# A graph-attention kernel: VectorE weights two gathered rows in two operations instead of one, and four products of TensorE's softmax chain get another form

## The reference

```python
def _gatv2_layer(x, src, dst, n, Wl, Wr, att, b):        # layers 0 and 1, with one self loop per node
    xl = (x @ Wl).reshape(n, H, C)
    xr = (x @ Wr).reshape(n, H, C)
    e = jax.nn.leaky_relu(xl[src] + xr[dst], NEG_SLOPE)
    logits = jnp.einsum('ehc,hc->eh', e, att)
    m = jax.ops.segment_max(logits, dst, num_segments=n)
    ex = jnp.exp(logits - m[dst])
    denom = jax.ops.segment_sum(ex, dst, num_segments=n)
    alpha = ex / (denom[dst] + 1e-16)
    msg = xl[src] * alpha[:, :, None]
    out = jax.ops.segment_sum(msg, dst, num_segments=n)
    return out.reshape(n, H * C) + b
...
    e = jax.nn.leaky_relu(s1[:, src] + s2[:, dst], ALPHA)   # layer 2: one score per node and head
    seg_max = jax.vmap(lambda x: jax.ops.segment_max(x, dst, num_segments=N))(e)
    ex = jnp.exp(e - seg_max[:, dst])
...
x = _layernorm(x + _L0_gnn_ref(...), axis=-1)
x = _layernorm(x + _L1_gnn_ref(...), axis=-1)
```

## Time and profile before

| | |
|---|---|
| median of three runs | 4111.03 us (4109.16 to 4114.46) |
| the profiled execution | 4120.86 us, its span 4119.0 us |
| mean granted TensorE clock | 0.948 |
| PE busy | 3664.7 us (89%), 31817 instructions |
| DVE busy | 3151.0 us (76%), 8749 instructions |
| POOL busy | 2738.6 us (66%), 2941 instructions |
| ACT busy | 1229.3 us (30%), 4200 instructions |
| L1558, the weighting | 1248 instructions, 856.2 us |
| L692, the gathers | 2496 instructions, 2545.3 us |

### The profile page before, as it was taken

How to read it: one execution, slowest core, us unless ns; L and a number is a source line. 1 busy time by engine, 2 the same in 40 slices (tenths; PEclk the granted TensorE clock), 3 DMA queues, 4 the chain that set the end, 5 groups by cost and what they waited for, 6 DMA issues and landing times. The chain is left out here.

```text
span 4119.0 us, 121901 instructions
## 1 busy us (share of the span) xinstructions
PE 3664.7 (89%) x31817; PEld 2727.4 (66%) x31818; DVE 3151.0 (76%) x8749; ACT 1229.3 (30%) x4200; POOL 2738.6 (66%) x2941
## 2 busy tenths in 40 slices
PE   6699999999999898999999999977788877887785
PEld 5577777777776676777777777745455555555553
DVE  6767877788778665788787787875688878887886
ACT  4433333333333563333333333323110111111113
POOL 5577777777775127777777777723777777777760
PEclk9899999999999999999999999989798888888889
DMA  4354444444443225444444444435555544544544
GB/s 98 108 141 130 132 131 132 126 133 131 131 126 98 62 66 136 134 131 132 126 133 131 130 128 133 125 107 177 137 135 138 139 132 136 138 136 132 137 107 125
DMA packets 333900, 521.05 MB, mean 126 GB/s; under 512 B 152888, under 2 KB 219618, under 8 KB 333810
## 3 DMA queue, kind: packets, MB, share of 16 engines
q0 software_dynamic: 120320, 338.39, 29.9%
q1 hardware_dynamic: 213489, 181.58, 15.5%
HBM read 484.14 MB, written 35.46 MB: 126 GB/s over the span
## 5 line engine op out<-in xcount | busy, mean ns | idle before, releaser
L692 POOL DMA_INDIRECT gathered<-table,idx x2496 | 2545.3, 1020 | 864.4 <-issue 519.3
L1131 PE MATMUL pS<-gathered,Dm 128*128 128x264 f32 x4992 | 1712.2, 426 | 92.8 <-DVE Dm L1541 48.3
L1528 DVE TENSOR_TENSOR acc_mem<-acc_mem,pS 128x264 f32 x2496 | 1039.6, 417 | 133.0 <-PE pS L1131 111.8
L1068 PEld LDWEIGHTS pZ<-DT,x 128*128 x9984 | 868.6, 99 | 338.3 <-issue 60.3
L1068 PE MATMUL pZ<-DT,x 128*128 128x128 bf16 x9984 | 1083.3, 221 | 10.4 <-DVE DT L1488 8.8
L853 ACT ACTIVATE reluT<-pZ 128x256 f32<-128x256 f32 x1664 | 637.0, 383 | 1301.4 <-PE pZ L1074 1283.2
L1131 PEld LDWEIGHTS pS<-gathered,Dm 128*128 128x128 f32 x4992 | 796.8, 201 | 236.2 <-DVE gathered L1558 115.4
L1074 PE MATMUL pZ<-ident,gathered 128*128 128x128 f32 x3328 | 936.8, 281 | 15.5 <-DMA gathered<-table,idx 15.3
L1558 DVE TENSOR_TENSOR gathered<-gathered 128x512 f32<-128x512 f32 x1248 | 856.2, 686 | 64.2 <-ACT gathered L870 63.2
L1541 DVE TENSOR_TENSOR Dm<-pS,rel_items 128x256 f32<-128x256 f32 x1239 | 512.6, 414 | 0.0
L1074 PEld LDWEIGHTS pZ<-ident,gathered 128*128 128x128 f32 x3328 | 471.6, 142 | 19.7 <-DMA gathered<-table,idx 18.0
(11 more groups left out here) (232 smaller groups left out, 3382.0 us busy)
## 6 DMA issues: line engine op xcount, KB each, us to landing
DT<-rel_dram SPq DMA_DIRECT2D x156, 512.0 KB
gathered<-table,idx POOLq DMA_INDIRECT x2496
flags<-flag_dram SPq DMA_DIRECT2D x1664, 8.0 KB
span_row<-flag_dram SPq DMA_DIRECT2D x1664, 0.1 KB
table<-xls SPq DMA_DIRECT2D x147, 132.0 KB, 1.9
flags<-flag_dram SPq DMA_DIRECT2D x416, 32.0 KB
gathered<-table SPq DMA_DIRECT2D x98, 132.0 KB, 2.1
gathered<-in_x SPq DMA_DIRECT2D x98, 128.0 KB, 2.1
```

Of the source, the lines that this page charges most:

```text
L692: nc.gpsimd.indirect_dma_start(out=G[:, b, i, :], out_offset=None, in_=tab[l], in_offset=bass.IndirectOffsetOnAxis(ap=idx[:, b, i:i + 1], ...
L1068: mm = nc.tensor.matmul(z_slot(i)[:, half], x3[:, bass.ds(tk[i], 1), s, half].rearrange("p o c -> p (o c)"), moving, start=(s == 0), stop= ...
L1131: nc.tensor.matmul(pS[:, i % 4, 0:ROW], Dm[:, i % 8, :], G[:, at[0], at[1], :], start=True, stop=True).then_inc(seg_done, 1)
L1528: link(v.tensor_tensor(acc_at(n), acc_at(n), pS[:, n % 4, 0:ROW], ALU.add))
```

## The change

VectorE: the one operation over two rows (2 x 256 elements per partition) becomes two operations over one row each (256 elements), directly behind each other; the second one signals `wg_done`. TensorE: the product with `lin` is marked as a transpose (`is_transpose=True`); of `F1` and `B1` only the first column is transposed, to one partition; the two products with one column each that turn `carry_in` become one product with two columns (`carry_in` now has one row for each direction, on partitions 0 and 32, in one tile, and the moving operand is columns 0 and 32 of the identity); and the transposes of `dif` and `mT` stand ahead of `expand(6)` instead of behind it.

```diff
-        carry_in = sb("carry_in", [P, 2, 8 * GI])
+        carry_in = sb("carry_in", [P, 8 * GI])
...
                     for i in range(GI):
                         freed = (l < 2 or i % 4 == 0) and (late if i <= GI // 2 else second)
+                        if second and i == 6:
+                            pe.wait_ge(dif_ready, up(dif_ready))
+                            nc.tensor.transpose(pM[:, P:2 * P], dif[:], ident[:])
+                            nc.tensor.transpose(pM[:, 0:P], mT[:], ident[:]).then_inc(dif_turned, 1)
                         if first and l < 2:
                             expand(i, freed)
                         if second and i == 0:
...
-                            nc.tensor.matmul(pL[:, 0:P], lin[:], ident[:],
+                            nc.tensor.matmul(pL[:, 0:P], lin[:], ident[:], is_transpose=True,
                                              start=False, stop=True).then_inc(logits_done, 1)
...
-                                nc.tensor.transpose(pM[:, 0:P], F1[:], ident[:])
-                                nc.tensor.transpose(pM[:, P:2 * P], B1[:], ident[:]).then_inc(ends_turned, 1)
+                                nc.tensor.transpose(pM[0:1, 0:P], F1[:, 0:1], ident[:])
+                                nc.tensor.transpose(pM[0:1, P:2 * P], B1[:, 0:1], ident[:]).then_inc(ends_turned, 1)
...
-                                for r in range(2):
-                                    mm = nc.tensor.matmul(pM[:, 256 + r:257 + r], carry_in[:, r, :], ident[:, 0:1], start=True, stop=True)
-                                mm.then_inc(carry_turned, 1)
-                            if i == 6:
-                                pe.wait_ge(dif_ready, up(dif_ready))
-                                nc.tensor.transpose(pM[:, P:2 * P], dif[:], ident[:])
-                                nc.tensor.transpose(pM[:, 0:P], mT[:], ident[:]).then_inc(dif_turned, 1)
+                                nc.tensor.matmul(pM[:, 256:258], carry_in[:], ident[:, 0:33:32], start=True, stop=True).then_inc(carry_turned, 1)
...
-                            two = G[:, at[0], at[1]:at[1] + 2, :]
-                            gv = two[:, :, 0:D].rearrange("p i (h d) -> p i h d", h=H)
-                            v.tensor_tensor(gv, gv, two[:, :, D:D + H].unsqueeze(3).to_broadcast([P, 2, H, D // H]), ALU.mult).then_inc(wg_done, 1)
+                            for k in range(2):
+                                row = G[:, at[0], at[1] + k, :]
+                                gv = row[:, 0:D].rearrange("p (h d) -> p h d", h=H)
+                                ins = v.tensor_tensor(gv, gv, row[:, D:D + H].unsqueeze(2).to_broadcast([P, H, D // H]), ALU.mult)
+                            ins.then_inc(wg_done, 1)
...
-                                    ins = v.tensor_copy(carry_in[0:1, r, :].rearrange("o (h k) -> o h k", h=H), row)
+                                    ins = v.tensor_copy(carry_in[32 * r:32 * r + 1, :].rearrange("o (h k) -> o h k", h=H), row)
                                 else:
-                                    ins = v.tensor_copy(heads_first(carry_in[0:1, r, :]), in_turns(row))
+                                    ins = v.tensor_copy(heads_first(carry_in[32 * r:32 * r + 1, :]), in_turns(row))
```

## The result

| | before | after |
|---|---|---|
| median of the runs | 4112.7 us (4109.2 to 4123.4) | 4093.95 us (4088.5 to 4096.8) |
| ratio | | 0.9945, 95% interval 0.9935 to 0.9956 |
| span of the profiled execution | 4119.0 us | 4095.0 us |
| layer 0, first to last `lin` product | 1103.0 | 1112.3 (+9.3) |
| layer 1 | 1104.3 | 1110.0 (+5.7) |

The forecast was 4063 us: 48 less, of which 34 in layer 2 and 14 in the other two. Measured were 19 less by the medians. The two profiled executions differ by 24 us: 45.5 won in layer 2 and 21.5 lost elsewhere (the layers' lengths are worked out from the starts of `lin` in the timelines).

The account below looks back on a forecast made before the run. TensorE was taken to bound layers 0 and 1, GpSimd's gather issue layer 2. Gains of 34 us (layer 2) and 14 us (layers 0 and 1) made 48 off 4111, so 4063 us, range 4025 to 4106.

Parts of the forecast that it names:

- GpSimd full in layer 2, the group 16 x (gather + 0.30): Layer 2 lasts as long as GpSimd takes to issue 832 gathers, each with a 0.30 us step; 21.73 us a group.
- The port, and the hold that ends with the first half: Layer 2: a running weighting holds gathers that start under it; split, the hold falls from 0.55 to 0.29 us.
- Size of layer 2: Shorter holds from the split weighting win 0.65 us in each of 52 groups: 34 us (16 to 54).
- VectorE as the bound: Rival: in layer 2 the eight pairs cost 1.92 us, over VectorE's 1.68 of idle time; 4117 us, chance 0.07.
- halves as one: Rival: a waiting gather gets in only behind the second half, held 0.63 us instead of 0.55; 4116 us, chance 0.08.
- `dif` late: Rival: TensorE waits 0.2 us for `dif` ahead of `expand(6)`, taking the gain of layers 0 and 1; 4083 us, chance 0.07.
- the clock: Rival: TensorE's clock stays at the low level in layer 2, 23.5 us a group instead of 21.7; 4191 us, chance 0.06.
- What is left is 0.44 - 0.22 - 0.08 = 0.14 us a group: Layers 0 and 1: TensorE's savings less moved transposes and longer split weighting; 14.6 us won over 104 groups.
- The lower bound of this term, a loss of 9 us: Layers 0 and 1: -0.09 us a group if `lin` and the carry give back half of what was taken.

Follow-up runs that it names:

- f1: Kernel before, with layer 2's weighting (one operation) reading its factor from PSUM, where ScalarE writes the exponentials a second time: 4057.4 us against 4115.6, ratio 0.9861.
- h1: Kernel before, with only VectorE's weighting split into two operations: 4114.4 us against 4113.6, ratio 1.000.
- i3: Changed kernel, with the transposes of `dif` and `mT` left behind `expand(6)`: 4067.0 us against 4117.5 for the kernel before, ratio 0.9872.
- i2: Changed kernel, with the weighting left in one operation (TensorE's products and the moved transposes only): 4164.9 us against 4117.5 for the kernel before, ratio 1.0112.

## Why the prediction was half right

- **GpSimd full in layer 2, the group 16 x (gather + 0.30)**: right, in all six kernels.
- **The port, and the hold that ends with the first half**: right. f1 shows the cause; 0.09 us measured where 0.10 was worked out for a gather 0.19 us behind the start, and 204 of 216 gathers under a first half were let in at 0.29 us. The Trainium skill's inferred sentence in "SBUF — State Buffer", section "Who interferes with whom", that a tensor_tensor leaves descriptor generation alone, does not hold for this instruction: with its factor moved out of SBUF the ratio is 0.9861. The other part of that section, that the one which issues first keeps the pair and the other is blocked, holds in one direction: the weighting that comes first blocks the gather. A weighting that starts behind a gather is not blocked: 463 such weightings of the kernel before take 0.68 us, those without a gather beside them 0.69.
- **Size of layer 2**: 34 us forecast, 45 measured. The split gives 27.6 (h1), less than forecast. The rest, 17.9, comes with the products (i3 has it without the move), which I had priced at nothing there, since I took the starts of gathers against weightings as given. They aren't: with the split the products lower the mean gather (1016 to 993 ns), with the long weighting products and move raise it (1053 to 1069). That the sum of layer 2 came out near its forecast is in part luck.
- **VectorE as the bound, halves as one, `dif` late, the clock**: none of them. The pairs take 0.67 us, VectorE still idles 22.3 us in 39 groups ahead of L1568, only 11 of 216 gathers were held by both halves, and the granted clock of layer 2 rose from 0.88 to 0.91. At L1089 TensorE waits 0.6 us in all 51 groups of layer 0; in layer 2 it waits 0.28 us in each (0.11 before), where GpSimd and not TensorE is full.
- **Layers 0 and 1, the step that failed.** "What is left is 0.44 - 0.22 - 0.08 = 0.14 us a group" had three terms, each off to the same side. In steady groups (from the sixth on) the period is 21.64 us before, 21.81 with the split alone, 21.45 with the products added and 21.71 with the move added; f1, which changes nothing in these layers, has 21.64 too. So the products give 0.36 and not 0.44: the carry gives its 0.22, but `lin` 0.16 and not 0.22, since as a transpose it still keeps TensorE 0.16 and not 0.11. The split costs 0.16 and not 0.08: 0.05 at the wait for the weighting, and 0.10 at `expand(4)`, for which the sum had no term. The move costs 0.26 and not 0.22. Together -0.06 where +0.14 stood. The lower bound of this term, a loss of 9 us, held for the steady groups (104 x 0.06 = 6). The three prices hold for this order of adding only: with the long weighting, products and move together cost 0.31 (21.95, i2), where in this order they give 0.10.
- **What the sum had no term for**: the first five groups of layers 0 and 1, 5.7 and 3.3 us longer, with the idle time of 4.7 us on VectorE, and 6.5 us between the layers, where nothing was changed and whose cause I don't know. Together 15.5 us, against 20.8 (14.6 forecast won, 6.2 lost) by which the steady groups were off. The stall alone doesn't make the first groups longer: i3 has it too, and its first five groups are 2.9 us longer and 1.9 shorter.

The move was the mistake of the change itself: the prediction had its price (0.22 us on the path) and no gain for it, and the sum stayed a gain only by the other two terms, 0.44 and 0.08, which measured 0.36 and 0.16.

## What to carry to other kernels

Where an engine is full and another's instruction holds its port, look for the input that can leave SBUF before you cut the instruction: that took 58 us off, the cut by itself none. When two engines run at nearly the same period, expect a shorter chain on one to move it against the other, and measure the parts in pairs: here -1 and -47 us made +19. A term of 0.1 us a group is not known from rows of one group: here three terms of this size were all off to the same side. Bound the sum with all of them at their worse end at once.

## What was not expected of the hardware

- An operation with one tensor input, in bf16, holds a gather just as well. VectorE and GpSimd of f1:

```profile
3400.27 0.75 DVE L1490 TENSOR_SCALAR DT<-DT,iota_part 128x2048 bf16<-128x2048 bf16 x1
```

```profile
3400.47 1.37 POOL L692 DMA_INDIRECT gathered<-table,idx  x1 [0.30 <-issue]
```

  The gather begins 0.20 us behind the spread of the relative positions and takes 0.42 longer. Once the weighting is out of the way this is the largest hold left in f1: 28 gathers between 3000 and 3900 us, 0.32 us each.
- The copies into `carry_in`, once one of them writes partition 32, follow each other at 0.22 and 0.24 us. Before, with both on partition 0, they stand 0.11 and 0.10 apart. VectorE before:

```profile
803.89 0.20 DVE L1585 COPY carry_in<-Fout 1x64 f32<-1x64 f32 x1
804.00 0.21 DVE L1585 COPY carry_in<-Bout 1x64 f32<-1x64 f32 x1
804.10 0.41 DVE L1528 TENSOR_TENSOR acc_mem<-acc_mem,pS 128x264 f32 x1
```

  VectorE after:

```profile
813.16 0.20 DVE L1585 COPY carry_in<-Fout 1x64 f32<-1x64 f32 x1
813.38 0.21 DVE L1585 COPY carry_in<-Bout 1x64 f32<-1x64 f32 x1
813.62 0.43 DVE L1526 TENSOR_TENSOR acc_mem<-acc_mem,pS 128x264 f32 x1
```

- The same program takes 4115 us on some chips and 5244 to 5331 on others, with instructions of the same length.
